# Loads of the last phase: one semaphore per kind of data, issued when their own buffer is free, and two transfers left out

## The reference, cut to what matters

```python
attn = softmax(q @ k.T) @ v                 # 16 heads of width 16
y    = xn + attn @ Wo + bo
ffn  = y + relu(layer_norm(y) @ W1 + b1) @ W2 + b2
shared = new_gelu(xn @ Wfc_s + bfc_s) @ Wproj_s + bproj_s
routed = sum over the 2 chosen experts of gate * expert(xn)
out  = x + ffn + shared + routed
```

## Time and profile before

| | us |
|---|---|
| median of 3 runs | 4233.71 |
| lowest, highest | 4231.51, 4236.89 |
| the profiled execution | 4234.2 |
| its span, first to last instruction | 4232.4 |
| mean granted TensorE clock | 0.976 |
| PE busy | 4045.8 (96%) |
| VectorE busy | 3147.5 (74%) |
| ACT busy | 2713.9 (64%) |
| start of the tail | about 3778 |

### The profile page before, as it was taken

One profiled execution on the slowest core, in us unless ns is written; L12 is line 12 of the kernel. 1 busy time (PEld: TensorE's weight loads), 2 busy tenths in 40 slices (PEclk: granted clock), 3 DMA queues, 4 the chain that ended last, 5 costly groups with the idle time before them and its releaser, 6 DMA issues. The chain is left out here.

```text
span 4232.4 us, 74482 instructions
## 1 busy us (share of the span) xinstructions
PE 4045.8 (96%) x27844; PEld 1866.3 (44%) x27844; DVE 3147.5 (74%) x4621; ACT 2713.9 (64%) x5153; POOL 370.7 (9%) x435
## 2 busy tenths in 40 slices
PE   6988788999999999999999999999999999997799
PEld 4666543222222222222222222222226888875566
DVE  6888568999999999999999999999960111132432
ACT  4555414888888888888888888888895232321112
POOL 0222332001101100000000000000000000011110
PEclk8999899999999999999999999999999999999899
DMA  4222464000014100003100002000002666632320
GB/s 157 80 87 89 144 127 68 26 19 18 22 34 67 53 21 4 4 7 55 32 7 4 4 6 75 4 6 4 4 6 86 220 213 209 213 123 69 90 60 31
DMA packets 213030, 269.66 MB, mean 64 GB/s; under 512 B 25152, under 2 KB 176448, under 8 KB 211168
## 3 DMA queue, kind: packets, MB, share of 16 engines
q1 hardware_dynamic: 200368, 236.85, 19.3%
q0 software_dynamic: 12336, 28.48, 2.5%
HBM read 188.43 MB, written 76.55 MB: 63 GB/s over the span
## 5 line engine op out<-in xcount | busy, mean ns | idle before, releaser
L1346 ACT ACTIVATE a_PT<-a_PS 128x512 f32<-128x512 f32 x4096 | 2163.7, 606 | 347.7 <-PE a_PS L1141 317.4
L1489 DVE TENSOR_REDUCE a_MX<-a_PS 128x1 f32<-128x512 f32 x2958 | 1889.1, 685 | 21.4 <-PE a_PS L1122 5.5
L1152 PE MATMUL a_OT<-a_PT,a_VG 128*32 128x512 f32 x8192 | 1093.0, 605 | 1.1 <-ACT a_PT L1346 0.7
L1484 DVE TENSOR_REDUCE a_MX<-a_PS 128x2 f32<-128x1024 f32 x569 | 692.1, 1218 | 25.9 <-PE a_PS L1122 24.9
L1141 PE MATMUL a_PS<-p_Q,p_K 64*128 64x512 bf16 x4096 | 688.6, 379 | 9.3 <-DVE a_MX L1489 7.4
L1141 PE MATMUL a_PS<-a_QS,h_K 64*128 64x512 bf16 x4096 | 675.3, 378 | 0.5 <-ACT a_PT L1346 0.5
L1122 PE MATMUL a_PS<-h_K,a_QS 64*128 64x512 bf16 x2048 | 505.0, 379 | 0.6
L1122 PE MATMUL a_PS<-p_K,p_Q 64*128 64x512 bf16 x2048 | 498.7, 381 | 3.8 <-DVE a_MX L1484 2.7
L1141 PEld LDWEIGHTS a_PS<-p_Q,p_K 64*128 64x128 bf16 x4096 | 226.7, 94 | 604.4 <-DVE a_MX L1489 266.0
L1141 PEld LDWEIGHTS a_PS<-a_QS,h_K 64*128 64x128 bf16 x4096 | 220.8, 94 | 590.3 <-ACT a_PT L1346 270.3
L1650 ACT ACTIVATE e_hT<-e_up,p_Q 128x256 f32<-128x256 f32 x312 | 147.7, 473 | 394.2 <-PE e_up L1604 394.0
(11 more groups left out here) (238 smaller groups left out, 3425.8 us busy)
## 6 DMA issues: line engine op xcount, KB each, us to landing
p_K<-Wfc SPq DMA_DIRECT2D x26, 1024.0 KB, 5.0
p_K<-Wproj SPq DMA_DIRECT2D x26, 1024.0 KB, 7.1
p_Q<-Wfc SPq DMA_DIRECT2D x13, 1024.0 KB, 5.4
p_Q<-Wproj SPq DMA_DIRECT2D x13, 1024.0 KB, 7.5
scr_xs<-f_zero SPq DMA_DIRECT2D x1, 9984.0 KB, 33.1
p_Q<-scr_xs SPq DMA_DIRECT2D x39, 256.0 KB, 2.7
scr_ys<-e_Y SPq DMA_DIRECT2D x39, 256.0 KB, 2.2
scr_va<-f_va SPq DMA_DIRECT2D x8, 1024.0 KB, 4.9
```

What stands on the lines that cost most here:

```text
L1152: last = T.matmul(OT[w, :], VG[j][:, u, w], PT[:, (n * CHUNKS + HG * u + i) % RING, :], start=u == 0, stop=u == KT - 1)
L1346: nc.scalar.activation(PT[:, at % RING, :], bank, ACT.Exp, scale=SOFT_SCALE).then_inc(S["exp_done"], 1)
L1484: V.tensor_reduce(MX[n % 2][:, :, x], PS[:, bank:bank + SIDES, :], AX.X, ALU.max).then_inc(S["mp_free"], SIDES)
L1489: V.reduce_max(MX[n % 2][:, side, x:x + 1], PS[:, bank, :], AX.X).then_inc(S["mp_free"], 1)
```

## The change

Each kind of load has a semaphore for each buffer (`sum`, `xn`, `res`, `xt`), and each wait asks only for the kind that it reads. SP issues for block i first SUM and DEN, once `att_ready` shows that block i-2's were read; then XN1, once block i-2's Y steps are done; then, if the block isn't SHARED, xT; then the store of block i-2; and last RES. Blocks 2 and 3 no longer load xT. VectorE waits for RES where it first adds to it. Blocks 0 and 1 are loaded as before, under a new function name.

```diff
-def rows_load(tt, i):
-
-    return (tt[f"early{i}"], TAIL_IN * 16) if i < 2 else (tt[f"load{i % 2}"], i // 2 * TAIL_IN * 16)
+def there(tt, name, i):
+
+    if i < 2:
+        return tt[f"early{i}"], TAIL_IN * 16
+    each = 2 * NG if name == "sum" else 1
+    rows = [n for n in range(2 + i % 2, i + 1, 2) if name != "xt" or n not in SHARED]
+    return tt[f"{name}{i % 2}"], len(rows) * each * 16
...
+def load_sums(eng, scr, tt, i, G, sem):
     j, n = i % 2, slice(i * BLK, (i + 1) * BLK)
+    rows, k = slice(G % 2 * HALF, (G % 2 + 1) * HALF), G // 2
+    heads = scr["att"][G].rearrange("(h w) n -> h w n", h=HG)
+    eng.dma_start(tt["SUM"][j][rows, k, :], heads[:, 0:HD1, n]).then_inc(sem, 16)
+    eng.dma_start(tt["DEN"][j][rows, k, :], heads[:, HD1:HD1 + 1, n].to_broadcast([HG, HD1, BLK])).then_inc(sem, 16)
+
+
+def load_block(eng, scr, tt, i, name, src, sem):
+    eng.dma_start(tt[name][i % 2][:], scr[src][i * BLK:(i + 1) * BLK, :].rearrange("(t p) c -> p t c", p=P)).then_inc(sem, 16)
+
+
+def load_turned(eng, scr, tt, i, sem):
+    eng.dma_start(tt["xT"][i % 2][:], scr["xn1T"][:, i * BLK:(i + 1) * BLK].rearrange("(c p) n -> p c n", p=P)).then_inc(sem, 16)
...
             for i in range(2, NB):
+                j = i % 2
+                sp.wait_ge(tt["att_ready"], (i - 1) * DC)
+                for G in range(NG):
+                    load_sums(sp, scr, tt, i, G, tt[f"sum{j}"])
+                sp.wait_ge(S["w_drained"], 2 * (i - 1))
+                load_block(sp, scr, tt, i, "XN1", "xn1", tt[f"xn{j}"])
+                if i not in SHARED:
+                    if i - 2 not in SHARED:
+                        sp.wait_ge(S["a_filled"], use_up(i - 2, HC - 1) + 1)
+                    load_turned(sp, scr, tt, i, tt[f"xt{j}"])
                 put(i - 2)
-                tail_rows(sp, scr, tt, i)
+                load_block(sp, scr, tt, i, "RES", "resid", tt[f"res{j}"])
...
                 if u == 0:
-                    pe.wait_ge(*rows_load(tt, i))
+                    pe.wait_ge(*there(tt, "xt", i))
...
-                dve.wait_ge(*rows_load(tt, i))
+                dve.wait_ge(*there(tt, "xn", i))
...
                 if i + 1 < NB:
-                    dve.wait_ge(*rows_load(tt, i + 1))
+                    dve.wait_ge(*there(tt, "sum", i + 1))
                     for k in range(DC):
                         attended(dve, V, tt, i + 1, k)
+                dve.wait_ge(*there(tt, "res", i))
                 c.step(V.tensor_tensor(RES[j][:], RES[j][:], Y[:], ALU.add))
```

More of the change, by code:

```diff
@@ L1565, in _ @@
             for i in range(2):
-                tail_rows(pool, scr, tt, i, lambda k: tiles_begun(TAIL_ROWS + (NTILE - TAIL_ROWS) * (i * TAIL_IN + k) // (2 * TAIL_IN)))
+                first_rows(pool, scr, tt, i, lambda k: tiles_begun(TAIL_ROWS + (NTILE - TAIL_ROWS) * (i * TAIL_IN + k) // (2 * TAIL_IN)))
         @block.sync
@@ L1680, in _ @@
                     if j == 0:
-                        dve.wait_ge(*rows_load(tt, 0))
+                        dve.wait_ge(*there(tt, "sum", 0))
                     attended(dve, V, tt, 0, j)
@@ L1697, in sb @@
         return ctx.enter_context(nc.sbuf_tensor("t_" + name, shape, dt))
-    tt = semaphores(nc, ctx, "t", "w_load early0 early1 load0 load1 att_ready att_chain")
+    tt = semaphores(nc, ctx, "t", "w_load early0 early1 sum0 sum1 xn0 xn1 res0 res1 xt0 xt1 att_ready att_chain")
     tt["wo"] = sb("wo", [P, DC, D])
@@ L1727, in tail_weights @@
         eng.dma_start(dst[:], src).then_inc(tt["w_load"], 16)
-def rows_load(tt, i):
-    return (tt[f"early{i}"], TAIL_IN * 16) if i < 2 else (tt[f"load{i % 2}"], i // 2 * TAIL_IN * 16)
-def tail_rows(eng, scr, tt, i, ready=lambda k: None):
-    j, n = i % 2, slice(i * BLK, (i + 1) * BLK)
-    there = rows_load(tt, i)[0]
+def there(tt, name, i):
[4 more added lines that the diff above has]
+    return tt[f"{name}{i % 2}"], len(rows) * each * 16
@@ L1738, in tail_rows, with first_rows @@
+def load_turned(eng, scr, tt, i, sem):
+    eng.dma_start(tt["xT"][i % 2][:], scr["xn1T"][:, i * BLK:(i + 1) * BLK].rearrange("(c p) n -> p c n", p=P)).then_inc(sem, 16)
+def first_rows(eng, scr, tt, i, ready):
+    sem = tt[f"early{i}"]
     for G in range(NG):
-        rows, k = slice(G % 2 * HALF, (G % 2 + 1) * HALF), G // 2
-        heads = scr["att"][G].rearrange("(h w) n -> h w n", h=HG)
         ready(2 * G)
-        eng.dma_start(tt["SUM"][j][rows, k, :], heads[:, 0:HD1, n]).then_inc(there, 16)
@@ L1743, in tail_rows @@
[L1743 to L1747, removed]
+        load_sums(eng, scr, tt, i, G, sem)
+    ready(2 * NG)
@@ L1750, in attended @@
+    load_block(eng, scr, tt, i, "XN1", "xn1", sem)
+    ready(2 * NG + 1)
+    load_block(eng, scr, tt, i, "RES", "resid", sem)
+    load_turned(eng, scr, tt, i, sem)
 def attended(dve, V, tt, i, k):
```

## The result

The changed kernel takes 4182.75 us (median of 4 runs, 4181.35 to 4183.05) against 4233.12 (4 runs, 4231.51 to 4236.89): 50.4 us less, a ratio of 0.9879 with a 95% interval of 0.9862 to 0.9896. The forecast was 4182.8.

The account below looks back on a forecast made before the run. TensorE bounds the kernel, idle at three tail gaps before projections because SUM and DEN loads queue behind a store. Removing 22.08 + 21.26 + 7.61 = 50.95 us from the profiled 4234.2 gives 4183.25, as median 4182.8; range 4178 to 4194.

Parts of the forecast that it names:

- Terms: PE's gaps and slow projections before blocks 2, 3 and 4 vanish: 22.08, 21.26 and 7.61 us, sum 50.95.
- The walk: Tail followed block by block through blocks 2 to 4: attT ready before PE wants it, so all three gaps go.
- VectorE ahead by 1.5 us: In blocks 2 and 3 VectorE finishes attT 1.5 us before PE wants it for the projection.
- Rival (b): VectorE becomes the bound in blocks 2 and 3; a step 3.5 us longer gives 4187 to 4191; chance 0.05.
- Is SUM(3) there: Block 3's SUM, issued from 3849, lands by 3869.4 even at 21.3 us; VectorE asks at 3881.5; cost zero.
- Rival (a): The transfer is late although issued a block earlier; costs 9.8 us of block 3's gain, 4192.6; chance 0.05.
- the order of semaphore writes: Skill rule: SUM(3)'s semaphore lands only behind earlier writes of the same DMA engine, put(0) and RES(2); sum unchanged.
- Part 2: No xT loads for blocks 2 and 3, two DMAs of 512 KB less: zero by itself.
- Part 3: Waits and order on SP's queue, with store and RES behind the other loads: hidden, taken as zero.
- Rival (c): SP still holds SUM(3) behind a store that ends too late, put(1): block 3's 21.26 us stay, 4204; chance 0.02.
- Rival (d): New transfers at 3778 delay GpSimd's gathers; 27 us hide, slower from 78 us, 4246 at 90 us; chance 0.01.

Follow-up runs that it names:

- the ten added instructions: The changed kernel with ten more VectorE instructions right before the reciprocals of each of blocks 2 and 3; 4190.2 us in one run.
- the wait for RES: The changed kernel, but VectorE's wait before the next block's reciprocals takes that block's RES as well as SUM; 4195.22 us, ratio 0.9911 to the kernel before.
- the kernel with semaphores alone: The changed kernel's semaphores and waits, but all eleven loads of a block issued at the old place behind the store; 4220.53 us, ratio 0.9967 to before.

## Why the prediction was right

**Terms.** Forecast 22.08 + 21.26 + 7.61 = 50.95, measured 50.95 on the same path. It comes out to the hundredth because every piece was a row of before, shifted; nothing was estimated except that SUM would be there. That the median (4182.75) met the forecast (4182.8) to 0.05 us is luck: the executions of before lie up to 5.4 us apart, and its own median moved by 0.6 when the fourth of them was added.

**The walk.** Turn of Z in block 2 at 3874.8, measured 3874.48; projection of block 3 at 3891.1, measured 3890.56; of block 4 at 3938.3, measured 3937.63. The differences are about the overlap of some 0.17 us at each warm start and the 0.18 by which the projection of block 1 was earlier.

**VectorE ahead by 1.5 us** in blocks 2 and 3: 1.56 by the ten added instructions, 1.48 by the wait for RES (5.58 - 4.10), and no gap when VectorE was about 0.7 us later. Rival (b) was therefore a real neighbour, but its price was too high: I gave a gap of 2 us up to 2.2 us of slow projection, and at 1.78 us the runs showed 0.10.

**Is SUM(3) there.** It was charged with the whole bundle of 21.3 us. In the changed kernel's own trace, the busy tenths of the DMA engines from 3845 to 3875 us in 40 slices and the issue of XN1(3) with its 11.6 us to landing are:

```profile
DMA  0000099459522337983222222220000031614426
t_XN<-scr_xn SPq DMA_DIRECT2D x1, 512.0 KB, 11.6
```

XN1(3), issued at 3854.78 behind all SUM and DEN loads, has landed at 3866.4, and SUM and DEN at 3865.0 (their last semaphore step), 17.2 us behind the issue of the store. VectorE asks at 3881.0: the 12 us of slack were in truth 16. Rival (a) is out for this kernel. What stood ahead, put(0) and RES(2), had landed by 3853.4, and the landings were in the order of issue. So the order of semaphore writes that the prediction set against separate semaphores made no difference here, and no run tests it by itself.

**Part 2 at zero:** shown by the kernel that keeps xT. **Part 3 at zero:** no DMA, and so neither a store nor RES, appears in a wait of PE or VectorE in the tail of the changed kernel. **Rival (c)** was run for its one block: it costs 16.2 us, not the 21.26 that I gave, since SUM on its own semaphore shortens the gap by 4.85 us (14.17 for 19.02) and the slow projection was 0.19 us faster. **Rival (d):** VectorE's sums of block 0 start without a wait in the changed kernel (at 3801.36), so the gathers beside the new transfers were in time, and Y of block 1 follows behind 19.94 us of idle time that is waiting for PE.

**What was off** without touching the sum: the first projection of the tail took 6.50 us instead of 5.38, after 3.3 us of idle time that the change doesn't touch. It was 6.5 to 6.65 us in most of the other kernels and 5.38 in two. The granted clock in that stretch was 0.57 in the changed kernel and 0.68 before; why the upper level came later isn't settled here.

## What to carry to other kernels

A load that stands behind a store in one in-order queue starts when the store's data are ready, not when its own buffer is free; ask for each buffer who read it last, and put the loads whose reader is done in front. Separate semaphores are what makes that possible when one of the bundle (here RES) can't be early, and here were worth a quarter of the gain alone. Where the path's engine is full in the later stages and idle only at named gaps, the sum of those gaps and of the slow work behind them, walked through once in order to see what is next late, was here the gain to within a microsecond.

## What the runs showed of the hardware that I had not expected

- A copy whose first dimension is 4 was carried by four of the 16 DMA engines: a DMA share of about 0.2 while such copies ran alone, and four late steps on the semaphore for each. In the kernel with semaphores alone the last of SUM and DEN (1.05 MB in eight such copies) landed 16.84 us after the drain; in four copies with a first dimension of 8 it was 11.05.
- A wide load issued behind them lands in two parts. XN1(3) of the changed kernel had twelve of its sixteen steps within 4.8 us of its issue and the last four only after 10.6 to 11.6 us, when the four engines were done with the narrow loads. In the kernel with semaphores alone RES(2) shows the same: twelve steps by 3858.1, the last four from 3863.3 to 3864.1, 13.8 us after its issue.
- The projection behind a gap: 3.72 us after gaps of 1.03 and 1.78; after longer ones 6.39 (3.62), 5.31 (4.10), 5.62 (5.44), 5.37 and 5.20 (9.57, 9.48), 5.50 (14.17), 6.50 and 6.52 (15.36, 14.80), 5.64 and 5.69 (19.89, 19.02). From 3.62 us on, the price is 1.6 to 2.9 us and doesn't follow the length of the gap. It goes with the granted clock in the projection's stretch: 1.00 at 3.72 us, 0.71 to 0.67 at 5.20 to 5.50, 0.65 at 5.62 to 5.69, 0.58 and 0.56 at 6.39 to 6.52.
